# AdaLN transformer block on one core: attention in blocks of two units, three shared PSUM banks, denominators and normalisation of a pair in the next block

## What is computed

```
h = layernorm(x) * (1 + ca) + sa
q, k, v = h @ Wq, h @ Wkv[:, :1024], h @ Wkv[:, 1024:]
s = (q / 8) @ k.T                       # per head, 256 x 256
p = where(causal_mask, 0, exp(s - rowmax(s)))
o = (p @ v) / (rowsum(p) + 1e-8)
x = x + ga * (o @ Wo + bo)
h = layernorm(x) * (1 + cb) + sb
gate, y = fp4(h) @ fp4(w_gate).T, fp4(h) @ fp4(w_up).T
x = x + gb * (fp4(silu(gate) * y) @ fp4(w_down).T)
```

## Time and profile before

| what | value |
|---|---|
| median of 3 runs | 1408.5 us (1407.82 to 1409.19) |
| the profiled execution | 1407.76 us, its span 1405.9 us, mean granted TensorE clock 0.982 |
| PE busy | 1333.2 us, 95% of the span |
| DVE, ACT, POOL busy | 974.4 us (69%), 998.4 us (71%), 846.4 us (60%) |
| chain that ended last | PE 72%, issue 9%, DVE 9%, ACT 8%, POOL 1%, DMA 1% |
| DMA | 6.4% of the 16 engines' time, 19 GB/s |

### The profile page before, as it was taken

How to read it: one execution, slowest core, us unless ns; L and a number is a source line. 1 busy time by engine, 2 the same in 40 slices (tenths; PEclk the granted TensorE clock), 3 DMA queues, 4 the chain that set the end, 5 groups by cost and what they waited for, 6 DMA issues and landing times.

```text
span 1405.9 us, 34736 instructions
## 1 busy us (share of the span) xinstructions
PE 1333.2 (95%) x10194; PEld 1008.6 (72%) x10194; DVE 974.4 (69%) x2405; ACT 998.4 (71%) x3301; POOL 846.4 (60%) x1582
## 2 busy tenths in 40 slices
PE   5999999999999999999999999999999999999974
PEld 3677777777777777777777777777777777777753
DVE  5557776677776677767677767677777677777664
ACT  3877777777777777767777777777777777777750
POOL 1556556666656666655666655666655666655653
PEclk7999999999999999999999999999999999999995
DMA  3000000000000000000000000000000000000000
GB/s 97 16 18 16 11 21 21 17 21 16 12 16 21 17 21 19 15 11 21 17 21 21 15 9 21 17 21 21 15 9 21 17 21 21 15 9 17 17 18 10
DMA packets 38057, 26.54 MB, mean 19 GB/s; under 512 B 2800, under 2 KB 33392, under 8 KB 38032
## 3 DMA queue, kind: packets, MB, share of 16 engines
q1 hardware_dynamic: 38032, 26.23, 6.4%
HBM read 21.94 MB, written 4.28 MB: 19 GB/s over the span
## 4 chain that ended last, share of the span: by engine, by line
PE 72%; issue 9%; DVE 9%; ACT 8%; POOL 1%; DMA 1%; ACTq 0%; SPq 0%; DVEq 0%; POOLq 0%
PE ps_m L796 18%; PE ps_s L883 17%; PE ps_t L775 13%; PE ps_m L833 8%; PE ps_o L906 7%; DVE probs_t L765 4%; PE ps_s L892 4%; ACT probs L546 4%; PE ps_m L857 3%; PE ps_m L775 2%; DVE neg_max L753 2%; ACT h_r L528 1%; DVE den_eps L759 1%; ACT probs_t L556 1%; ACT hq_t L523 1%
## 5 line engine op out<-in xcount | busy, mean ns | idle before, releaser
L546 ACT ACTIVATE probs<-ps_s,neg_max 128x128 f32<-128x128 f32 (+1 forms) x1024 | 424.1, 430 | 77.5 <-PE ps_s L892 77.5
L753 DVE TENSOR_REDUCE neg_max<-ps_s 128x4 f32<-128x1024 f32 x256 | 311.6, 1217 | 77.0 <-PE ps_s L883 69.9
L426 POOL TENSOR_SCALAR probs<-probs,r_den 128x256 f32<-128x256 f32 (+1 forms) x768 | 350.1, 471 | 0.0
L775 PE MATMUL ps_t<-ident,probs 128*128 128x128 f32 x1536 | 274.1, 287 | 31.8 <-DVE probs_t L765 15.6
L883 PE MATMUL ps_s<-qk 64*128 64x256 f32 x2048 | 291.5, 403 | 0.0
L424 POOL TENSOR_TENSOR probs<-probs,r_den 128x128 f32<-128x128 f32 x256 | 107.8, 421 | 299.8 <-DVE r_den L762 290.4
L775 PEld LDWEIGHTS ps_t<-ident,probs 128*128 128x128 f32 x1536 | 158.8, 140 | 114.9 <-issue 86.9
L514 ACT COPY qk<-ps_m 128x512 f32<-128x512 f32 x256 | 152.4, 595 | 112.5 <-PE ps_m L796 112.5
L906 PE MATMUL ps_o<-probs_t,v 128*64 128x256 f32 (+1 forms) x2048 | 223.0, 339 | 1.1 <-ACT o_t L537 0.7
L546 ACT ACTIVATION_READ_ACCUMULATOR probs<-ps_s,neg_max 128x1 f32 x1024 | 219.6, 214 | 0.0
L883 PEld LDWEIGHTS ps_s<-qk 64*128 64x128 f32 x2048 | 176.9, 186 | 54.6 <-issue 27.3
(11 more groups left out here) (108 smaller groups left out, 1898.3 us busy)
## 6 DMA issues: line engine op xcount, KB each, us to landing
mod_a<-mod_rows SPq DMA_DIRECT2D x32, 256.0 KB, 3.3
x_in<-L_attn_x SPq DMA_DIRECT2D x32, 128.0 KB, 2.1
x_res<-L_attn_x SPq DMA_DIRECT2D x32, 128.0 KB, 2.1
out<-y_out SPq DMA_DIRECT2D x32, 128.0 KB, 1.8
mod_b<-mod_rows SPq DMA_DIRECT2D x32, 64.0 KB, 2.8
wkv<-L_attn_Wkv SPq DMA_DIRECT2D x2, 512.0 KB, 7.0
wq<-L_attn_Wq SPq DMA_DIRECT2D x1, 512.0 KB, 4.0
wo<-L_attn_Wo SPq DMA_DIRECT2D x1, 512.0 KB, 8.4
```

Source lines behind the costliest of these rows:

```text
L426: ins = nc.gpsimd.tensor_scalar(cols, cols, r_den[:, par, s:s + 1], 1.0, ALU.mult, ALU.mult)
L546: ins = nc.scalar.activation(probs[:, u % 4, h, t * P:(1 + 2 * t) * P], ps_s[:, 2 * par + h, t * N:t * N + (1 + t) * P], ACT.Exp, bias=neg ...
L753: nc.vector.tensor_reduce(neg_max[:, par, :], ps_s[:, 2 * par:2 * par + 2, :].rearrange("p b (t j) -> p (b t) j", t=2), AX.X, ALU.max, neg ...
L775: return nc.tensor.transpose(dst, src, ident[0:n, 0:n])
```

## The change

Every engine's body becomes a loop over `PAIRS` = 4 blocks `j` of two units. Within a block:

- PE issues both `scores`, then `values(j)` for the two units of pair `j-2`, the masks of the first unit, place 0, place 1, the masks of the second unit, and places 2 to 8.
- The transposes of the probabilities are no longer steps of their own with the bank `ps_t`. The twelve 128x128 pieces of a pair become three groups of four, kind `"t"`, at places 0, 2 and 5 of the next block, in the shared banks. `ps_t` is gone, and `ps_m` has three banks, taken in turn. Groups 0 and 1 are copied by DVE, group 2 by ACT (`T_ON_ACT`), 512 columns each. The other shared steps get new places.
- DVE computes `den_eps` and `r_den` of both units of a pair at once, as the first thing of the next block (`denominators(j - 1)`), ahead of that block's maxima. The maxima of both units follow.
- POOL normalises both units of the previous pair first in each block, and the side work comes behind: `xq` is rounded in block 0 of the next iteration (before: in unit 7), `x1_keep` behind it, `round_hidden` in blocks 2 and 3 behind the normalisation.
- DVE's side work is spread over the blocks. The quantisation of `h2` is the last thing of block 3, behind the reads of both `down` steps (before: in unit 6, ahead of them).
- ACT does the second unit's exponentials in two parts around place 4 and 5; `out_copy` moves two units at once, in block 1 right behind the first unit's exponentials, else at the end of the block.
- SP issues its DMAs at block 1 (`mod_b`), 2 (`x_in`) and 3 (`x_res`, `mod_a`, `out`), with the same waits.

The diff, cut to the placing of the steps and the order on POOL, ACT, DVE and PE:

```diff
+        PLACES = {
+            (0, 3): ("xqt", 2, 0), (0, 4): ("v", 0, 0), (0, 7): ("gate", 2, 0), (0, 8): ("up", 2, 0),
+            (1, 3): ("wo", 1, 0), (1, 4): ("gate", 2, 1), (1, 7): ("v", 0, 1), (1, 8): ("up", 2, 1),
+            (2, 3): ("wo", 1, 1), (2, 4): ("v", 0, 2), (2, 7): ("v", 0, 3), (2, 8): ("xt", -1, 0),
+            (3, 3): ("hqt", 2, 0), (3, 4): ("hqt", 2, 1), (3, 7): ("down", 2, 0), (3, 8): ("down", 2, 1)}
+        for j in range(PAIRS):
+            for g, n in enumerate((0, 2, 5)):
+                PLACES[j, n] = ("t", 0, 3 * (j - 1) + g) if j > 0 else ("t", 1, 3 * (PAIRS - 1) + g)
+            for k, n in enumerate((1, 6)):
+                PLACES[j, n] = ("qk", 0, 2 * (j + 1) + k) if j < PAIRS - 1 else ("qk", -1, k)
+        assert len(PLACES) == 9 * PAIRS
+
+        WEIGHT_PLACES = [(0, 7), (0, 8), (1, 4)]
...
+        T_ON_ACT = (2,)
...
+                for j in range(PAIRS):
+                    if has.unit(2 * j - 1):
+                        normalize(i, 2 * j - 2)
+                        normalize(i, 2 * j - 1)
+                    if j == 0 and has.prev2:
+                        pool.wait_ge(xq_steps, QUANT_STEPS * (i - 1))
                         if not isinstance(i, int) or i > 2:
-                            pool.wait_ge(y_ready, 2 * (i - 2))
-                        pool.wait_ge(wo_scaled, 2 * (i - 1))
-                        nc.gpsimd.tensor_tensor(x1_keep[:, :, :], attn[:, :, :], x_gb[:, :, :], ALU.add).then_inc(kept, 1)
-                    if u == 1 and has.prev:
+                            pool.wait_ge(xqt_full, i - 2)
+                        quantize_round(nc.gpsimd, Steps(pool, xq_round, ROUND_STEPS, i - 2), xq, 2 * P // BLOCK, scale[0],
...
+                    if j in (2, 3) and has.prev2:
+                        round_hidden(i - 2, j - 2)
+                    if j == 3 and has.prev:
...
-                    if u == 7 and has.prev:
-                        pool.wait_ge(xq_steps, QUANT_STEPS * i)
-                        if has.prev2:
-                            pool.wait_ge(xqt_full, i - 1)
-                        quantize_round(nc.gpsimd, Steps(pool, xq_round, ROUND_STEPS, i - 1), xq, 2 * P // BLOCK, scale[0],
-                                       qy[0], qm[0])
...
-                    if has.unit(u - 1):
-                        normalize(i, u - 1)
+                        quantize_round(nc.gpsimd, Steps(pool, weights_round, done=j - 1), wfq, WB // BLOCK, scale_w,
+                                       qy_w, qm_w, parts=(j - 1,))
+                    if j == 0 and has.prev2:
+
+                        if not isinstance(i, int) or i > 2:
+                            pool.wait_ge(y_ready, 2 * (i - 2))
...
+                        if j == 2 and has.prev:
+                            act.wait_ge(wo_full, 2 * i)
+                        at = 2 * ((j - 2) % PAIRS)
+                        act.wait_ge(o_full, PAIRS * i + j - 1)
...
+                    has_out = has.unit(2 * (j - 2))
+                    if has.attn:
+                        exponentials(2 * j, 0)
+                        exponentials(2 * j, 1)
+                    if has_out and j == 1:
                         out_copy()
-                    if has.unit(u - 2) and u in PT0_ON_ACT:
-                        act.wait_ge(pt_full, 16 * i + 2 * (u - 2) + 1)
-                        nc.scalar.copy(probs_t[:, u % 2, 0, :], ps_t[:, 0:3 * P]).then_inc(pt0_ready, 1)
-                    shared_reads(u, "a")
-                    if has.unit(u - 2):
-                        act.wait_ge(pt_full, 16 * i + 2 * (u - 2) + 2)
-                        nc.scalar.copy(probs_t[:, u % 2, 1, :], ps_t[:, 0:3 * P]).then_inc(pt1_ready, 1)
-                    shared_reads(u, "b")
+                    for n in (0, 1, 2, 3):
+                        shared_reads(n)
                     if has.attn:
-                        exponentials(0)
-                    shared_reads(u, "c")
-                    if has.unit(u - 3) and u in OT_LATE:
-                        if has.prev:
-                            act.wait_ge(wo_full, 2 * i)
+                        exponentials(2 * j + 1, 0)
+                    shared_reads(4)
+                    shared_reads(5)
+                    if has.attn:
+                        exponentials(2 * j + 1, 1)
+                    for n in (6, 7, 8):
+                        shared_reads(n)
+                    if has_out and j != 1:
                         out_copy()
...
+                def denominators(j):
+                    two = slice(2 * (j % 2), 2 * (j % 2) + 2)
+                    dve.wait_ge(exp_done, 16 * i + 4 * j + 4)
+                    nc.vector.tensor_scalar(den_eps[:, two, :], den[:, two, :], SOFTMAX_EPS, None,
+                                            ALU.add).then_inc(eps_added, 1)
+                    dve.wait_ge(eps_added, PAIRS * i + j + 1)
+                    nc.vector.reciprocal(r_den[:, two, :], den_eps[:, two, :]).then_inc(rden_ready, 1)
+
+                for j in range(PAIRS):
+                    if has.unit(2 * j - 1):
+                        denominators(j - 1)
+                    if has.attn:
+                        maxima(2 * j)
+                    if j == 3 and has.next:
+
+                        dve.wait_ge(ht_ready, 2 * (i + 2))
+                        nc.vector.tensor_tensor(h_r[1][:, :], h_t[:, :], h_r[0][:, :], ALU.subtract).then_inc(hr_ready, 1)
+                    if has.attn:
+                        maxima(2 * j + 1)
+                    shared_reads(j, 0)
+                    shared_reads(j, 2)
...
+                    shared_reads(j, 7)
+                    shared_reads(j, 8)
+                    if j == 3 and has.prev:
...
+                for j in range(PAIRS):
                     if has.attn:
+                        scores(2 * j)
+                        scores(2 * j + 1)
+                    if has.unit(2 * (j - 2)):
+                        values(j)
                     if has.attn:
+                        mask(2 * j, 0)
+                        mask(2 * j, 1)
+                    at_place(j, 0)
+                    at_place(j, 1)
                     if has.attn:
+                        mask(2 * j + 1, 0)
+                        mask(2 * j + 1, 1)
+                    for n in range(2, 9):
+                        at_place(j, n)
 
             iterations(pe, body)
```

More of the change, by code:

```diff
@@ L373, in body @@
                 has = Has(i)
-                for u in range(UNITS):
-                    if i_is(i, 0) and u == 3:
+                for j in range(PAIRS):
+                    if i_is(i, 0) and j == 1:
                         sp.wait_ge(setup_dve, SETUP_ROWS)
@@ L379, in body @@
                         sp.wait_ge(rows_out, 16)
[L380 removed]
+                    if j == 1 and has.prev2:
                         if not isinstance(i, int) or i > 2:
@@ L508, in body, with shared_reads @@
                 shared = shared_steps(i)
-                for u in range(UNITS):
-                    def shared_reads(u, place):
-                        kind, b, k, bank, _ = shared.get((u, place), (None, 0, 0, 0, None))
-                        if kind == "qk":
+                for j in range(PAIRS):
+                    def shared_reads(n):
+                        kind, b, k, bank, _ = shared.get((j, n), (None, 0, 0, 0, None))
+                        if kind == "t" and k % 3 in T_ON_ACT:
+                            act.wait_ge(pt_full, 3 * PAIRS * b + k + 1)
+                            nc.scalar.copy(probs_t[:, 4 * (k % 3):4 * (k % 3) + 4, :],
+                                           ps_m[bank][:, :].rearrange("p (c j) -> p c j", c=4)).then_inc(pt_ready[k % 3], 1)
+                        elif kind == "qk":
                             act.wait_ge(qk_full, UNITS * b + k + 1)
@@ L638, in body, with shared_reads @@
                 shared = shared_steps(i)
-                def shared_reads(u, place):
-                    kind, b, k, bank, _ = shared.get((u, place), (None, 0, 0, 0, None))
-                    if kind == "weights":
+                def shared_reads(j, n):
+                    kind, b, k, bank, _ = shared.get((j, n), (None, 0, 0, 0, None))
+                    if kind == "t" and k % 3 not in T_ON_ACT:
+                        dve.wait_ge(pt_full, 3 * PAIRS * b + k + 1)
+                        nc.vector.tensor_copy(probs_t[:, 4 * (k % 3):4 * (k % 3) + 4, :],
+                                              ps_m[bank][:, :].rearrange("p (c j) -> p c j", c=4)).then_inc(pt_ready[k % 3], 1)
+                    elif kind == "weights":
                         dve.wait_ge(weights_full, k + 1)
@@ new lines, in body @@
+                for j in range(PAIRS):
+                    if has.unit(2 * j - 1):
[9 more added lines that the diff above has]
+                    shared_reads(j, 2)
+                    if j in (1, 2) and has.prev2:
+                        hidden_scales(i - 2, j - 1)
+                    if j == 3 and has.prev:
```

(4 more changed lines are left out.)

217 lines of the change are left out of this document (86 added, 131 removed), and 4 rows, old and new, of the table PLACES.

## The result

The changed kernel takes **1499.24 us** (median of 4 runs, 1496.47 to 1503.13) against 1408.16 us of the kernel before: ratio 1.065, 95% interval 1.0624 to 1.0676. The forecast was 1520 us, range 1485 to 1578. It is slower, as forecast, by 91 us instead of 111.

The account below looks back on a forecast made before the run. PE bounds the kernel, with 1.0 us of waiting per batch. Waits of 5.05 us instead, less 0.4 of denser matmuls, give +3.65 us; over 30.5 batches 111 us, so 1520 us, range 1485 to 1578.

Parts of the forecast that it names:

- Theory A: Task order on DVE and POOL makes PE wait; in block 0 xqt starts 9.3 us after first scores, not 5.9.
- xqt: Block 0: PE's transposes of xq wait 1.95 us per batch for POOL's rounding, now behind two normalisations.
- hqt(1): Block 3, place 4: PE waits 0.9 us per batch for POOL's round_hidden(1), which follows the normalising.
- values(3): Block 2: PE waits 0.1 us per batch for the copy behind xt.
- four changes between masks and scores: PE, per batch: four of eight such changes go, taking 0.4 us off its work, bounds 0 to 0.8.
- first masks: Block 0: PE's first masks wait 0.95 us per batch, because DVE's maxima start at 3.4 us instead of 1.2.
- t0 in block 0: PE's first group of probability transposes needs two normalised heads from POOL and waits 0.45 us per batch.
- block 1: PE waits 0.7 us per batch: 0.45 for ACT's copy ahead of wo, 0.25 at v for a bank.
- my 40.4: PE's dense work per batch in us, without waits; the forecast took 0.4 off for denser matmuls.
- The low clock: Rival: block 0's holes lower PE's clock, 1.2 us each (bounds 0 and 1.5), 1556 us if every batch; chance 0.22.
- The waits are hidden after all: Rival: xq is rounded before 5.7 us into block 0, PE has only dense work, 1357 us; chance of faster 0.03.
- Normalising was not slower: Rival: POOL's normalising slows beside DVE in blocks 0 and 3, 1565 us; chance 0.12, shared with further waits.

Follow-up runs that it names:

- e2: The changed kernel with one edit on POOL: in block 0 the rounding of xq stands ahead of the two normalisations; 1487.86 us, ratio 1.0564.

## Why the prediction was right, and where it was off

**The mechanism.** All of it was there. Theory A's decisive number was that `xqt` can start 9.3 us after block 0's first scores; the trace has 641.16 - 631.89 = 9.27. Denominators to normalising took 0.49 us, two normalisations 3.25, rounding 2.24 (against 0.45, 3.35 and 2.23 from the earlier trace rows). That the sum hits 9.3 is partly luck: the six quantising instructions, 632.57 to 634.59, took 2.02 us and not 2.24, and were done 0.4 us earlier than taken, but between them and the denominators DVE was idle for 0.54 us, for which the sum had no term. `hqt(1)`, `wo`, `values(3)` and the masks wait for those that were named. DVE's work grew by 21 us over the kernel, 0.7 per batch and not 3; nothing hung on that.

**PE's work was mis-sized.** I took 0.4 us per batch off the dense 40.8, for four changes between masks and scores. Measured, the dense work is 44.55 less 6.66 of waits (next point), 37.9 us: 2.9 off, and my bound of 0.8 was too small by 2. The step that failed counted one kind of change only, and took two units' scores as 2 x 1.06. Two in a row save 0.19 us at the scores and 0.17 at the values, 1.4 per batch in four blocks. The masks, of which the 0.4 was a guess, went from 2.33 to 1.83 us per batch, 0.5. Of the rest, 0.8 is the step from `qk` to the second group of transposes, 0.46 us in the kernel before and 0.36 now, eight times, and 0.3 the transposes themselves. Why these two are shorter was not tested.

**The waits were mis-sized the other way, for the same reason.** Counted from start to start less the undisturbed step (`xqt`: 641.16 - 638.48 - 0.43 = 2.25). Predicted and measured, us per batch: `xqt` 1.95 and 2.25; first masks 0.95 and 1.45; t0 in block 0 0.45 and 0.13; `hqt(1)` 0.9 and 1.6; block 1 0.7 and 0.73; `values(3)` 0.1 and 0.5. Sum 5.05 against 6.66. The times at which DVE and POOL deliver hardly moved, PE came earlier, and so it waits longer: a shorter list on an engine that waits for others is paid back at the next wait. Of the 2.5 us by which the dense work fell short of my 40.4, 1.6 went that way. At `hqt(1)` the normalising also began 1.4 us into the block, where I had 0.95.

**The sum.** The period grew by 2.62 us (41.93 to 44.55) where I had 3.65: over 30.5 batches 80 us in place of 111. Four long batches add some 6; the other 6 of the 92 us between the two spans lie in start, end and the batches that the 30.5 leaves out.

**The rivals.** The low clock, given 0.22 for many batches, came in four; its price, taken as 1.2 us with a bound of 1.5, is 1.5. The price was built on 3.0 us of low clock in two windows of 2 us; the low stretches here are 3.4 us. The holes that the Trainium skill (TensorE: Matmul & The Clock Gate, "Why this matters for your kernels") names as bringing the clock down are only those longer than about 3 us. The traces here do not agree that shorter ones are harmless: with no idle time of PE above 2.2 us in the steady part it fell in four batches, and with the quantisation moved in thirteen. "The waits are hidden after all", 1357 us, did not come by this change, but its price was near what the runs gave once the order was mended: 1359, and 1333 with ACT's order too. (1357 stood on a dense period of 40.4 us, so that it fits is partly luck.) That there was no room for it was true of the order as written, and not of the blocks. Normalising was not slower in block 0 (1.28 and 1.29 us for the three instructions of a unit); in block 3 the first unit took 1.45, the second 1.28.

## What to carry to other kernels

When an engine's list is regrouped, follow what it delivers, not what it does: write the chain from the last shared result to the first instruction that waits for it, with every task that stands ahead in each engine's order, and compare its end with the time at which the bottleneck arrives. Side work with a deadline belongs ahead of bulk work that has slack, on each engine that it crosses; moving one link gives little when the next stands in the same queue (13 and 11 us here, 24 and 13 by the undisturbed period), moving the chain gives what it cost (71). And a gain of the bottleneck's own work shows in the time only where nothing else is late.

## What the hardware did that I had not expected

- Changing between values (128 rows, 64 columns) and masks or transposes (128 x 128) costs PE about 0.13 us each time: 256 such changes more made 45 us on 1333, of which about 13 are waits of the masks for DVE. The tile's shape and the operands change together there, so which of them it is stays open. Waits that are already satisfied cost nothing at the same places (1333.76 against 1332.95 us).
- With a hole of 2.1 us on PE once per batch its clock fell from 2.4 to 1.2 GHz in 4, 12 or 13 of 29 batches, 1.5 us each; the kernel with 13 of them, given 1.6 us of matmuls in the hole that nobody reads, was 22 us faster and kept 2.4 GHz. With no hole above 1.6 us (e2) it fell in seven.
- DVE's copy of 512 columns out of PSUM, which no row of before showed, takes 0.69 us, ACT's 0.59 (page of the kernel after):

```profile
L655 DVE COPY probs_t<-ps_m 128x512 f32<-128x512 f32 x256 | 176.6, 690 | 141.1 <-PE ps_m L795 141.1
```
